# A three-step residual convolution and its linear attention on one core: projection, folded map and second 1x1 map as plain fp32 products

## The reference

```python
for _ in range(3):
    t = relu(conv(x, w1) + b1)
    x = x + (1/3) * (conv(t, w2) + b2)
x = relu(x)
```

```python
q, k, v = split(qkv_w @ x)                # per head, 8 channels each
k, v = ln(k), ln(v)                       # mean, and standard deviation with ddof=1
o = q @ ((k.T @ v) / N)                   # an 8x8 matrix per head
u = gelu(o1_w @ (o + x))
out = gelu(o2_w @ u + x)
```

## Time and profile before

| | us |
|---|---|
| two runs | 1805.56, 1811.71 |
| their median | 1808.63 |
| span of the profiled execution | 1808.4 |
| PE busy | 1760.9 (97%), 10875 matmul records |
| PEld busy | 1613.7 (89%) |
| DVE busy | 1268.9 (70%) |
| ACT busy | 916.9 (51%) |
| mean granted TensorE clock | 0.991 |

### The profile page before, as it was taken

The page is one execution under the profiler, slowest core; times in us unless marked ns, Lnnn a source line. Parts: engine busy times, 40 slices in busy tenths (PEclk is TensorE's granted clock), DMA queues, the critical chain, the costliest instruction groups (busy, mean ns, idle before and its releaser), DMA issues.

```text
span 1808.4 us, 30258 instructions
## 1 busy us (share of the span) xinstructions
PE 1760.9 (97%) x10875; PEld 1613.7 (89%) x10875; DVE 1268.9 (70%) x2481; ACT 916.9 (51%) x1533; POOL 1.8 (0%) x16
## 2 busy tenths in 40 slices
PE   7999999999999999999999999999999999999995
PEld 6998989989899898998989989898899989999884
DVE  4674668857687676876668676696666957679585
ACT  3453636446454464545545455454455545455473
POOL 0000000000000000000000000000000000000000
PEclk9999999999999999999999999999999999999997
DMA  3110002020021101111020110201102010000102
GB/s 56 27 22 0 1 1 48 13 36 3 16 33 24 24 3 25 30 19 24 3 41 14 18 25 1 47 7 24 20 1 48 13 24 13 1 1 13 30 7 47
DMA packets 135415, 36.17 MB, mean 20 GB/s; under 512 B 135116, under 2 KB 135116, under 8 KB 135244
## 3 DMA queue, kind: packets, MB, share of 16 engines
q1 hardware_dynamic: 135164, 33.82, 11.2%
q10 hardware_dynamic: 80, 0.15, 0.0%
HBM read 17.17 MB, written 16.78 MB: 19 GB/s over the span
## 4 chain that ended last, share of the span: by engine, by line
PE 87%; DVE 7%; issue 4%; ACT 1%; DVEq 0%; DMA 0%; ACTq 0%
PE bank L900 27%; PE bank L901 26%; PE bank L902 26%; PE bank L996 3%; PE bank L984 2%; PE bank L986 2%; PE bank L985 2%; DVE v_lo L770 1%; DVE combined L737 1%; DVE combined L741 1%; DVE combined L738 1%; DVE x_lo L770 1%; DVE combined L742 0%; DVE kv L793 0%; PE bank L1014 0%
## 5 line engine op out<-in xcount | busy, mean ns | idle before, releaser
L900 PE MATMUL bank<-x_hi,w_hi 128*128 128x448 f32 (+2 forms) x1440 | 517.2, 359 | 13.9 <-issue 7.4
L901 PE MATMUL bank<-x_lo,w_hi 128*128 128x448 f32 (+2 forms) x1440 | 511.4, 355 | 0.0
L902 PE MATMUL bank<-x_hi,w_lo 128*128 128x448 f32 (+2 forms) x1440 | 511.2, 355 | 0.0
L900 PEld LDWEIGHTS bank<-x_hi,w_hi 128*128 128x128 f32 x1440 | 273.2, 190 | 32.2 <-issue 12.6
L901 PEld LDWEIGHTS bank<-x_lo,w_hi 128*128 128x128 f32 x1440 | 273.4, 190 | 15.1
L902 PEld LDWEIGHTS bank<-x_hi,w_lo 128*128 128x128 f32 x1440 | 272.5, 189 | 15.3
L494 ACT ACTIVATE drain<-bank,b_col 128x448 f32<-128x448 f32 (+1 forms) x160 | 98.1, 613 | 254.7 <-PE bank L902 253.9
L500 ACT ACTIVATE drain<-bank 128x512 f32<-128x512 f32 x256 | 154.8, 615 | 107.3 <-PE bank L902 104.6
L719 DVE TENSOR_TENSOR combined<-drain 128x448 f32<-128x448 f32 (+1 forms) x160 | 95.8, 598 | 105.9 <-ACT drain L494 99.5
L770 DVE TENSOR_TENSOR v_lo<-combined,v_hi 128x896 fp32r<-128x896 f32 (+1 forms) x160 | 165.1, 1032 | 0.3
L900 PE MATMUL bank<-t_hi,w_hi 128*128 128x512 f32 x384 | 156.1, 407 | 0.0
(11 more groups left out here) (144 smaller groups left out, 3259.7 us busy)
## 6 DMA issues: line engine op xcount, KB each, us to landing
x_in<-in_x SPq DMA_DIRECT2D x64, 256.0 KB, 4.7
out<-y SPq DMA_DIRECT2D x120, 128.0 KB, 2.6
out<-drain SPq DMA_DIRECT2D x8, 128.0 KB, 2.7
x_res<-in_L_conv_w ACTq DMA_DIRECT2D x1, 144.0 KB, 2.9
x_res<-in_L_conv_w SPq DMA_DIRECT2D x1, 144.0 KB, 5.1
b_col<-in_L_conv_b SPq DMA_DIRECT2D x4, 0.2 KB, 3.0
g<-in_L_conv_o_w SPq DMA_DIRECT2D x3, 16.0 KB
g<-in_L_conv_qkv_w SPq DMA_DIRECT2D x2, 16.0 KB
```

The lines of the kernel that those rows point to most:

```text
L900: mm(ps, lhs[0], rhs[0], start=first, stop=False)
L901: mm(ps, lhs[0], rhs[1], start=False, stop=False)
L902: return mm(ps, lhs[1], rhs[0], start=False, stop=last)
```

## The change

The convolutions stay as they are. In the attention, the tiles `f_hi`/`f_lo`, `kvw_hi`/`kvw_lo`, `gw_hi`/`gw_lo`, `o2_hi`/`o2_lo` and `g_hi`/`g_lo` become single fp32 tiles `f`, `kvw`, `gw`, `o2` and `g`. Each triple of fp32r matmuls becomes one fp32 matmul. The instructions that wrote the second halves are gone: on DVE `f_lo` (line 766), `g_lo` (line 819), the low part of `gw` (line 814) and the second addition to `y` (line 837), and on ACT the second GELU (line 554). For the last step's chunks, DVE still waits for ACT's `hi_written` and then signals `conv_out`, with no work in between. DOWN waits for `gelu_done` in place of `g_split`.

```diff
-        f_hi = pair_of("f_hi", [P, PIX], F32R)
-        f_lo = pair_of("f_lo", [P, PIX], F32R)
+        f = pair_of("f", [P, PIX])
...
-                    nc.scalar.activation(f_hi[img][:, pixels], x_res[img][:, pixels], ACT.Relu
+                    nc.scalar.activation(f[img][:, pixels], x_res[img][:, pixels], ACT.Relu
                                          ).then_inc(hi_written, 1)
...
-                            act.wait_ge(g_split, done - 1)
                             act.wait_ge(down_ready, done - 1)
                         ps = ring_ps[uses.index(s) % RING]
-                        nc.scalar.activation(g[k % 2][:, :], ps[:, :], ACT.Gelu)
-                        nc.scalar.activation(g_hi[k % 2][:, :], ps[:, :], ACT.Gelu).then_inc(gelu_done, 1)
+                        nc.scalar.activation(g[k % 2][:, :], ps[:, :], ACT.Gelu).then_inc(gelu_done, 1)
...
-                    v.scalar_tensor_tensor(f_lo[img][:, pixels], x_res[img][:, pixels], 0.0,
-                                           f_hi[img][:, pixels].bitcast(F32), ALU.max, ALU.subtract
-                                           ).then_inc(conv_out, 1)
+                    dve.sem_inc(conv_out, 1)
                     return
...
-                                v.tensor_copy(gw_hi[img][rows, cols], gw_ps[rows, :]).then_inc(gw_hi_written, 1)
-                                dve.wait_ge(gw_hi_written, a * 4 + img * 2 + p + 1)
-                                low = v.tensor_tensor(gw_lo[img][rows, cols], gw_ps[rows, :],
-                                                      gw_hi[img][rows, cols].bitcast(F32), ALU.subtract)
-                            low.then_inc(small_taken, 1)
-                    elif kind == UP:
-                        dve.wait_ge(gelu_done, tail + 1)
-                        v.tensor_tensor(g_lo[k % 2][:, :], g[k % 2][:, :], g_hi[k % 2][:, :].bitcast(F32),
-                                        ALU.subtract).then_inc(g_split, 1)
+                                last = v.tensor_copy(gw[img][rows, cols], gw_ps[rows, :])
+                            last.then_inc(small_taken, 1)
...
-                        v.tensor_tensor(y[k % 2][:, :], ps[:, :], f_hi[img][:, at].bitcast(F32), ALU.add
-                                        ).then_inc(f_hi_added, 1)
-                        dve.wait_ge(f_hi_added, tail + 1)
-                        v.tensor_tensor(y[k % 2][:, :], y[k % 2][:, :], f_lo[img][:, at].bitcast(F32), ALU.add
-                                        ).then_inc(down_added, 1)
+                        v.tensor_tensor(y[k % 2][:, :], ps[:, :], f[img][:, at], ALU.add).then_inc(down_added, 1)
...
-                            mm(to, f_hi[img][:, at], kvw_hi[:, :], start=True, stop=False)
-                            mm(to, f_hi[img][:, at], kvw_lo[:, :], start=False, stop=False)
-                            last = mm(to, f_lo[img][:, at], kvw_hi[:, :], start=False, stop=True)
+                            last = mm(to, f[img][:, at], kvw[:, :], start=True, stop=True)
...
-                        three(ring_free(a, s, uses)[:, :], (gw_hi[img][:, :], gw_lo[img][:, :]),
-                              (f_hi[img][:, at], f_lo[img][:, at]),
-                              True, True).then_inc(up_ready, 1)
+                        mm(ring_free(a, s, uses)[:, :], gw[img][:, :], f[img][:, at],
+                           start=True, stop=True).then_inc(up_ready, 1)
                     elif kind == DOWN:
-                        pe.wait_ge(g_split, tail + 1)
-                        three(ring_free(a, s, uses)[:, :], (o2_hi[:, :], o2_lo[:, :]),
-                              (g_hi[k % 2][:, :], g_lo[k % 2][:, :]),
-                              True, True).then_inc(down_ready, 1)
+                        pe.wait_ge(gelu_done, tail + 1)
+                        mm(ring_free(a, s, uses)[:, :], o2[:, :], g[k % 2][:, :],
+                           start=True, stop=True).then_inc(down_ready, 1)
```

More of the change, by code:

```diff
@@ L248, in conv_attention_kernel @@
         squares = g
-        g_hi = pair_of("g_hi", [P, BANK], F32R)
-        g_lo = pair_of("g_lo", [P, BANK], F32R)
         y = pair_of("y", [P, BANK])
@@ L257, in conv_attention_kernel @@
         u_lo = sb("u_lo", [P, 2, 2, P], F32R)
[L258 to L263, removed]
+        kvw = sb("kvw", [P, 2 * KV])
+        gw = pair_of("gw", [P, P])
+        o2 = sb("o2", [P, P])
         b1_col = sb("b1_col", [P, 1])
@@ L335, in conv_attention_kernel @@
         small_ready = sem("small_ready")
-        gw_hi_written = sem("gw_hi_written")
         small_taken = sem("small_taken")
@@ L339, in conv_attention_kernel @@
         gelu_done = sem("gelu_done")
-        g_split = sem("g_split")
         down_ready = sem("down_ready")
@@ L343, in conv_attention_kernel @@
         y_ready = sem("y_ready")
-        f_hi_added = sem("f_hi_added")
         stored = [sem(f"stored{k}") for k in range(2)]
@@ L630, in split_x_lo @@
                                 x_hi[k][:, groups, 1:COLS + 1].bitcast(F32), ALU.subtract).then_inc(x_split, 1)
-            def split_small(hi, lo, value):
-                link(v.tensor_copy(hi, value))
-                return v.tensor_tensor(lo, value, hi.bitcast(F32), ALU.subtract)
             def set_up(n):
@@ L647, in set_up @@
                 if TAPS_AT.get(n) == 2:
-                    for w in (kvw_hi, kvw_lo, *gw_hi, *gw_lo, o2_hi, o2_lo):
-                        v.memset(w[:, :].bitcast(F32), 0.0)
+                    for w in (kvw, *gw, o2):
+                        v.memset(w[:, :], 0.0)
                     v.memset(kv_head[CH:ONE, :], 0.0)
@@ L670, in set_up @@
                         rows = slice(CH * p, CH * p + CH)
[L671 to L674, removed]
+                        v.tensor_copy(kvw[rows, KV * p:KV * p + KV], kvw_centred[rows, :])
+                        v.tensor_copy(o2[rows, CH * p:CH * p + CH], banks[7][rows, KV:KV + CH])
                     v.tensor_copy(o1_t[:, :], banks[7][0:CH, KV + CH:KV + 2 * CH]).then_inc(weights_split, 1)
```

## The result

The changed kernel took 1833.82 us (median of 2 runs, 1833.42 and 1834.21) against 1808.63 us before (1805.56 and 1811.71). The ratio is 1.0138, with a 95% interval of 1.0113 to 1.0162. So the change costs 1.4%, clear of noise and under 2%. The forecast was 1836 us, with 1822 to 1858 as the range. The profiled execution's span is 1831.3 us.

The account below looks back on a forecast made before the run. PE was taken to bound the kernel except in the last 60 us, where it waits for DVE and ACT. 1808.4 + 35.8 - 3.4 - 5.5 = 1835.3 us of span, forecast as 1836 us; range 1822 to 1858.

Parts of the forecast that it names:

- What bounds the kernel: PE sets the pace while convolutions run; in the last 60 us PE waits for DVE and ACT.
- The price of a long fp32 matmul: Attention products on PE: two records per matmul, 0.215 us each at 256 columns and 0.430 at 512.
- The upper bound from OUTER's stream: Highest price for fp32 on PE, from OUTER's 65-column records: 0.91 ns a column, 0.466 and 0.932 us a matmul.
- rival 1: On PE, each of four fp32 passes costs an fp32r pass: 1855.8 us, slower by 2.6%; chance 0.18.
- OUTER's 5 ns: Extra time in OUTER's short fp32 matmuls, taken as more likely a cost per record than per column.
- The lower bound: Lowest price on PE: an fp32 record streams at fp32r's pace, 0.240 and 0.460 us a matmul.
- rival 3: On PE, an fp32 record streams a column a cycle: 1743 us, faster by 3.6%; chance 0.05.
- The sum on PE: Before 1750 us: PROJECT +16.8 us, UP and DOWN +19.0, together +35.8.
- What DVE and ACT give back in the middle: OUTER's waits for NORMALISE in seven pairs go, 0.49 us each: -3.4 us.
- The end: From 1750 us: `f_lo` and PROJECT -1.8 us, FOLD's `gw` -1.0, UP and DOWN -2.7; together -5.5.
- The longer matmuls: In the end, UP and DOWN add 2.7 us on PE; 0.6 us shows of the longer last projections.
- Rival 2: The seven waits stay and longer matmuls eat the end's saving: 1848 us, slower by 2.2%; chance 0.17.

Follow-up runs that it names:

- e4: Changed kernel with three fp32r matmuls of the same rounded tiles per attention product in place of one fp32 matmul: 1796.77 us, ratio 0.9941.
- e5: Changed kernel with one fp32r matmul for each attention product, low parts left out: 1695.15 us, ratio 0.9382.
- e1: Kernel before with only PROJECT's triples as one fp32 matmul each, all DVE and ACT work kept: 1829.33 us, ratio 1.0118.
- e2: Kernel before with only UP's and DOWN's triples as one fp32 matmul each, DVE and ACT work kept: 1830.33 us, ratio 1.0130.
- e3: Changed kernel with all removed DVE and ACT work and its waits put back, low parts unread by PE: 1840.31 us, ratio 1.0185.
- e6: Kernel before with one fp32r matmul for each PROJECT triple only, DVE and ACT work kept: 1756.13 us, ratio 0.9728.
- e7: Kernel before with PE's loop over the six middle pairs written out, so no back edge: 1802.57 us, ratio 0.9982.
- e8: e5 with PE's loop over the six middle pairs written out as in e7: 1687.81 us, ratio 0.9346.

## Why the prediction was right

**What bounds the kernel.** Right. PE sets the pace in the middle. Giving back 150 us of DVE's and ACT's work (e4) bought 9 us by the medians, and taking two fp32r matmuls from each product (e5 against e4) bought 102.

**The price of a long fp32 matmul.** Right, and the point that decided. 0.215 and 0.430 us a record were read from one 64-column matmul and from fp32r at the lower clock; 0.216 and 0.430 were measured. The upper bound from OUTER's stream (0.91 ns a column) falls, and with it rival 1: at 0.91 ns 256 columns would take 0.233 us. Over two cycles a column (0.213 and 0.427 us) some 3 ns are left at 256 and at 512 columns, so OUTER's 5 ns are no cost per column, as the prediction supposed. What they are was not shown. The lower bound, and rival 3, fall by the same rows. The Trainium skill, "FP8 and Floating Point Precision", section "TensorE Precision Notes", counts four passes for true fp32. The trace agrees if a pass is one column a cycle: two records of two cycles a column. But four of fp32r's records would have taken 4 x 0.120 = 0.480 us for 256 columns, and the matmul takes 0.431. The rule gave the direction, and the rows the size.

**The sum on PE.** Nearly right. It was +35.8 us before 1750 us, 5.0 a middle pair. The changed kernel against e4 gives 222.64 - 217.87 = 4.8 us a pair, and e1 and e2 together 4.7. The small remainder lies in UP and DOWN: 2.52 us for 16 of them is 0.16 each, where 0.17 was counted; PROJECT's 2.20 for 32 is 0.07 each, as counted.

**What DVE and ACT give back in the middle.** Right, in place and in size. The seven waits of OUTER are gone. The forecast was 0.49 us each; less the gaps, e3 and e4 give 0.50 and 0.51 us a pair. With e3 the waits come back, so the cause is shown from that side. With e4 they only shrink to 0.20 us, and where the other 0.3 us of its pair come from was not shown.

**The end.** Forecast -5.5, and the stretch is 5.2 us shorter. That the sum came out is luck: two terms were too large and cancelled. The relief was put at 8.8 us and is 6.0 to 6.2 (e4, e3). Of its parts, PE's waits for `f_lo` fell from 1.78 to 0.23 us at the place that the forecast quotes. It did not name the longer one ahead of it, which fell from 2.23 to 0.82 us and belongs to the last pair's convolutions in the table below. So `f_lo` gave 2.9 us in all, with 2.4 forecast, and the bare signal that was costed at nothing keeps 1.1. The waits for `gw` fell from 2.1 to 1.1 us, as forecast. DOWN's waits for `g_lo` were only 2.4 us in three places and went; with the FOLD step's 0.9 that makes 3.3 us, where 5.4 was taken. The longer matmuls were put at 2.7 + 0.6 and cost 0.8 (after against e4): UP and DOWN stand largely in waits there. The granted clock of e4's end is 0.79 against 0.85 after, so the 0.8 may be too low.

**The total.** By the profiled spans the step is 1831.3 - 1808.4 = +22.9 us, where +26.9 was forecast. The stretches say where the 4 us lie (us, the forecast's terms put in the same places):

| | before | after | step | forecast |
|---|---|---|---|---|
| up to the loop's first matmul | 202.45 | 203.01 | +0.6 | 0 |
| the six middle pairs | 1322.94 | 1346.34 | +23.4 | +26.8 |
| the last pair's convolutions | 229.28 | 233.49 | +4.2 | +5.6 |
| the end | 53.72 | 48.49 | -5.2 | -5.5 |

Of the 3.4 us that the middle pairs lack, 1.5 are a stretch at the lower clock that the profile before has and the one after has not (two against one), 0.9 are shorter gaps at the back edge, and 1.1 are the small remainder in PE's term. The first two have nothing to do with the change. The 1.4 us that the last pair lacks match the wait for `f_lo` that fell from 2.23 to 0.82 us, which the forecast had put in the end. By the medians the step is +25.2 us, or +28 against the later runs of the kernel before; the forecast in these terms was +27.4. The 0.2 us that the prediction added from span to median joined two different executions; each run's time is about 2 us above its own span. Rival 2 (the relief does not come) falls by e3 and e4: put the old work back and the kernel is longer by 6.5 us in the medians and by 10.9 from the loop on.

## What to carry to other kernels

One fp32 matmul in place of three fp32r ones costs a fifth to a quarter more PE time (0.431 for 0.360 us at 256 columns, 0.860 for 0.690 at 512). Here it paid only where PE waits for the engines that make the split, in the kernel's last 50 us, and not where PE is full. Before a cost is moved from a half-idle engine to the full one, ask whether the split is needed: dropping the low parts of these three products, and with them their precision, was worth 110 us (e5). Before two profiles are compared pair by pair, take out what differs by itself: here the gap at the back edge and the stretches at the lower clock. With both out, terms of 0.5 us a pair can be read, while the medians were off by several microseconds. A price that the trace does not show at the right size can be had from a small instance, if what is loaded and what is streamed are taken apart first.

## What the runs showed of the hardware that I had not expected

**The clock behind the back edge.** The 2 us without a matmul at the end of a round are sometimes followed by a stretch at the lower of TensorE's two levels, and sometimes not. Stretches of the kernel before, 4 us each, behind such a gap; then the two pairs that hold them:

```profile
1079.00:1083.00 4.00, 2.11 (x18) 1.91 (x17) 3.86 (x9) 2.46 (x4) 0.00 (x0) 1.00 0.03 8
1083.00:1087.00 4.00, 3.95 (x12) 3.63 (x13) 2.70 (x6) 0.00 (x0) 0.00 (x0) 0.57 0.04 10
...
1083.05:1304.77 221.72, 219.34 (x1356) 201.33 (x1357) 157.42 (x305) 114.22 (x191) 0.00 (x0) 0.99 0.12 20
1304.77:1525.39 220.62, 219.37 (x1357) 201.37 (x1357) 156.41 (x303) 113.60 (x190) 0.00 (x0) 0.99 0.12 20
```

The granted clock is 1.00 in the stretch with the gap and 0.57 in the next. Less their gaps (1.89 and 0.80 us) the two pairs take 219.8 us in place of 218.4, so each such stretch costs 1.5 us. The profile before has two of them behind a back edge, after has one, e1 three, e2 and e5 two each, e4 one, e3 and e6 none. Without the back edge (e7, e8) there is none in the middle, and no middle pair is longer than another.

**The start is not the same twice.** The first matmul of the loop's first round starts at different times in kernels that have done the same convolutions until then. Timelines of PE of e3 and of e2, each followed by the stretch from 20 to 30 us:

```profile
199.41 0.47 PE L891 MATMUL bank<-x_hi,w_hi 128*128 128x448 f32 x1 [0.70 <-ACT drain L498]
20.00:30.00 10.00, 9.13 (x55) 8.68 (x56) 3.97 (x11) 2.93 (x7) 0.00 (x0) 1.00 0.01 2
```

```profile
203.79 0.48 PE L900 MATMUL bank<-x_hi,w_hi 128*128 128x448 f32 x1 [0.70 <-ACT drain L500]
20.00:30.00 10.00, 8.38 (x34) 7.58 (x35) 2.00 (x8) 1.05 (x3) 0.00 (x0) 0.66 0.01 2
```

That is 4.4 us before the attention has begun, and it goes with the clock. Of the ten profiles, the five with a granted clock of 1.00 between 20 and 30 us (e1, e3, e6, e7, e8) start the loop at 199.4 to 200.5 us, the five with 0.66 or 0.83 (before, after, e2, e4, e5) at 202.0 to 203.8. The runs say the same of the whole: of the 22 of the kernel before beside the experiments, the six with a mean granted clock of 0.994 span 1802.3 to 1804.1 us, the two with 0.989 span 1808.4 and 1812.0. Why the clock falls in one execution and not in the next was not shown. It is why terms of a few microseconds are read here from stretches and not from medians.

**fp32r does not stream a column a cycle at the full clock.** 256 columns take 0.120 us, 512 take 0.230, 0.45 to 0.47 ns a column, where 2.4 GHz gives 0.417. At the lower clock 256 columns take 0.215, which is one column a cycle. fp32, at two cycles a column, shows no such surplus at the full clock (0.216). This is why four passes cost 0.431 and not 0.480 us.

**Where a record starts.** The first fp32r record behind a long fp32 matmul looks very long, because it starts only some 0.03 us after the second fp32 record, so that most of it lies beside that one:

```profile
1226.53 1.08 PE L989 MATMUL bank<-f,gw 128*128 128x512 f32 x2
1227.04 0.75 PE L869 MATMUL bank<-x_hi,w_hi 128*128 128x384 f32 x1
1227.63 0.34 PE L870 MATMUL bank<-x_lo,w_hi 128*128 128x384 f32 x1
```

From the start of line 989's pair to that of line 870 are 1.10 us: the two fp32 records (0.86), one fp32r matmul of 384 columns (0.18), and 0.05 to 0.06 us that this row does not explain. If the change of type had a price of its own, e1 and e2 would show it in every pair; they show 0.07 and 0.16 us a product, no more than the longer matmuls account for. Only the idle and busy times of single groups are misread if one takes them by record.
